# Edges and node tiles taken from the last to the first in a graph-attention and mixture-of-experts kernel

## The reference

```python
def reference(x, src, dst, ...):
    n = layernorm(x)
    h = (n @ W).reshape(N, 8, 256)                      # 8 heads
    a_src, a_dst = einsum(h, att_src), einsum(h, att_dst)
    e = leaky_relu(a_src[src] + a_dst[dst], 0.2)
    alpha = softmax of e over the edges of each dst      # max, exp, sum, divide
    x = x + segment_sum(h[src] * alpha, dst).mean(heads) + bias
    t = layernorm(x)
    probs = softmax(t @ router_w.T); the top 2 of 8 experts, weights normalised
    return x + t + sum over the two of weight * (gelu(t @ w1[e] + b1[e]) @ w2[e] + b2[e])
```

## Time and profile before

| | |
|---|---|
| median of three runs | 1113.08 us |
| the profiled execution | 1112.33 us, its span 1110.6 us |
| busy share PE, DVE, ACT, POOL | 64%, 62%, 32%, 60% |
| granted TensorE clock, mean | 0.81 |
| first gather, first block, last block, last projection | 75, 213, 725, 932 us |

### The profile page before, as it was taken

One profiled execution on the slowest core, in us unless ns is written; L12 is line 12 of the kernel. 1 busy time (PEld: TensorE's weight loads), 2 busy tenths in 40 slices (PEclk: granted clock), 3 DMA queues, 4 the chain that ended last, 5 costly groups with the idle time before them and its releaser, 6 DMA issues.

```text
span 1110.6 us, 16896 instructions
## 1 busy us (share of the span) xinstructions
PE 708.7 (64%) x3738; PEld 629.2 (57%) x3739; DVE 688.1 (62%) x1906; ACT 359.7 (32%) x833; POOL 664.9 (60%) x687
## 2 busy tenths in 40 slices
PE   1594002427565454756676666679999998669884
PEld 0593001317455444745566565568888888558774
DVE  6888008737574674667578676536768865735452
ACT  4800003000111122333464565543223222426553
POOL 1668778777777777777777700134063265556665
PEclk9855555578868787887886886789999998979998
DMA  9523143333444455665676748489876761455663
GB/s 347 170 52 86 50 101 98 104 109 105 138 126 139 144 153 165 190 197 173 213 249 202 237 172 326 160 298 354 332 291 220 274 241 64 107 110 94 103 106 47
DMA packets 97065, 190.12 MB, mean 171 GB/s; under 512 B 24745, under 2 KB 54772, under 8 KB 95848
## 3 DMA queue, kind: packets, MB, share of 16 engines
q0 software_dynamic: 31632, 70.45, 25.4%
q1 hardware_dynamic: 50236, 72.80, 19.2%
q10 hardware_dynamic: 15072, 45.36, 10.9%
HBM read 124.74 MB, written 64.74 MB: 171 GB/s over the span
## 4 chain that ended last, share of the span: by engine, by line
PE 27%; POOL 22%; issue 16%; DMA 11%; DVE 10%; ACTq 6%; ACT 6%; POOLq 2%; DVEq 0%; SPq 0%
POOL ring L670 19%; PE banks L879 11%; PE banks L1000 10%; DMA out<-ring 6%; ACTq L1150 5%; POOL starts_table L725 2%; PE banks L854 2%; ACT banks L1168 1%; ACT arena L1164 1%; ACT ring L1121 1%; DMA ring<-agg_table 1%; DMA agg_table<-arena 1%; DMA ring<-node_table,idx 1%; ACT banks L1170 1%; PE banks L1020 1%
## 5 line engine op out<-in xcount | busy, mean ns | idle before, releaser
L670 POOL DMA_INDIRECT ring<-node_table,idx x392 | 409.3, 1044 | 125.7 <-issue 114.8
L879 PE MATMUL banks<-arena,ring 128*128 128x160 f32 x1568 | 289.5, 350 | 125.2 <-issue 60.8
L879 PEld LDWEIGHTS banks<-arena,ring 128*128 128x128 f32 x1568 | 268.8, 228 | 147.0 <-issue 147.0
L1164 ACT COPY arena<-banks 128x400 f32<-128x400 f32 x200 | 88.3, 492 | 292.3 <-PE banks L879 148.1
L782 POOL DMA_INDIRECT out<-ring x56 | 88.5, 1581 | 61.0 <-DMA out<-ring 28.4
L1000 PE MATMUL banks<-ring 128*128 128x256 f32 x544 | 120.5, 381 | 0.0
L1000 PEld LDWEIGHTS banks<-ring 128*128 128x128 f32 x544 | 102.5, 190 | 13.4
L1609 DVE TENSOR_TENSOR arena<-hot,arena 128x640 f32<-128x640 f32 x98 | 75.1, 821 | 38.8 <-PE banks L879 38.4
L1168 ACT COPY banks<-zeros 128x400 f32<-128x400 f32 x100 | 49.5, 495 | 89.2 <-ACT arena L1164 52.2
L1059 PEld LDWEIGHTS banks<-ring 128*128 128x128 f32 x448 | 61.5, 203 | 14.6 <-DVE ring L1837 11.9
L1075 PE MATMUL banks<-arena,ring 128*128 x224 | 64.3, 413 | 7.6 <-issue 4.9
(11 more groups left out here) (374 smaller groups left out, 1106.3 us busy)
## 6 DMA issues: line engine op xcount, KB each, us to landing
agg_table<-arena ACTq DMA_DIRECT2D x100, 400.0 KB
ring<-agg_table SPq DMA_DIRECT2D x25, 1600.0 KB, 8.0
ring<-slot_table SPq DMA_DIRECT2D x56, 130.0 KB, 2.4
ring<-node_table,idx POOLq DMA_INDIRECT x392, 3.2
ring<-in_x SPq DMA_DIRECT2D x8, 640.0 KB, 14.7
arena<-in_L_ffn_w SPq DMA_DIRECT2D x16, 256.0 KB, 8.9
node_table<-ring SPq DMA_DIRECT2D x5, 640.0 KB, 5.1
out<-ring POOLq DMA_DIRECT2D x5, 512.0 KB, 4.3
```

The lines of the kernel that those rows point to most:

```text
L670: pool.indirect_dma_start(rows[:, b % ROOM, :], None, node_table, bass.IndirectOffsetOnAxis(idx[:, b:b + 1], 0)).then_inc(got[got_of(g)], 16)
L879: m = pe.matmul(columns[:, k, bass.ds(at * (UNIT * H), SPREAD * H)], lhs[:, k * P:(k + 1) * P], weights, start=False, stop=True, skip_grou ...
L1164: act.copy(stage[j][:, k * SLOTS * H:(k + 1) * SLOTS * H], views[k]).then_inc(drained, 1)
```

## The change

Every key is mirrored: an edge's destination becomes 3199 - dst (`MIRROR`), edges and tiles run from last to first. Homes 0 and 1 are then the empty ones, home 2 holds the padding and the last nodes, home 99 holds nodes 0 to 31. The edges are reversed within rows as they are read, and the table of destinations is written by an indirect store on POOL in place of a plain one on ACT. `aggt` is written with both inner dimensions reversed, so that tiles come out in the usual lane order. `rows_of(t)` = 24 - t gives the tile of nodes of step t. The step of 53 real nodes is now the first, so the first ten steps have 1205 real nodes in place of 1280, and `FIRST_JOBS` falls from 13 to 11; `job_lists`, `job_rows` and `job_experts` of round two each stand one result earlier.

```diff
-FIRST_JOBS = 13
+FIRST_JOBS = 11
-STORE = 4
+BASE_STORES = ((1, 5), (5, 9), (9, 13), (13, 17), (17, 20))
+    MIRROR = TILES * P - 1
+        def rows_of(t):
+            return TILES - 1 - t
 # SP
             load_nodes(0)
+            sp.wait_ge(node_pad, 1)
+            sp.dma_start(x_all[0:LAST_WHOLE, FULL, :], x[FULL * P:FULL * P + LAST_WHOLE, :]).then_inc(in_nodes[0], 16)
+            sp.dma_start(x_all[LAST_WHOLE:LAST, FULL, :], x[FULL * P + LAST_WHOLE:N, :]).then_inc(in_nodes[0], 16)
...
+            sp.wait_ge(base_ready, 1)
+            sp.dma_start(out[FULL * P:FULL * P + LAST_WHOLE, :], x_all[0:LAST_WHOLE, FULL, :]).then_inc(end_stored, 16)
+            sp.dma_start(out[FULL * P + LAST_WHOLE:N, :], x_all[LAST_WHOLE:LAST, FULL, :]).then_inc(end_stored, 16)
 # POOL
+            link(pool.tensor_scalar(node_keys[:, :], node_ids[:, :], -1.0, float(MIRROR), ALU.mult, ALU.add))
+            link(pool.iota(row_places[:, :], ...))
+            pool.wait_ge(keys_ready, 1)
+            pool.indirect_dma_start(dst_table.rearrange("(i n) -> i n", n=RUN), ..., dst_keys, None).then_inc(dst_stored, 16)
 # ACT
-            act.wait_ge(in_edges, 16 * 2 * (1 + TURN_ROWS - TURN_WHOLE))
-            act.dma_start(dst_table.rearrange("(i n) -> i n", n=RUN), edges_i[:, 1, :]).then_inc(dst_stored, 16)
-                         bank[h][:, 0:NB].rearrange("p (r i) -> p r i", r=TURN_BLOCKS)).then_inc(score_d_ready, 1)
+                         bank[h][:, 0:NB].rearrange("p (r i) -> p r i", r=TURN_BLOCKS)[:, :, ::-1]).then_inc(score_d_ready, 1)
-                to = aggt[t % AGG_RING].rearrange("p (k h) (v n) -> p k h v n", k=2, n=HOME)
+                to = aggt[t % AGG_RING].rearrange("p (k h) (v n) -> p k h v n", k=2, n=HOME)[:, :, :, ::-1, ::-1]
 # DVE
-            dve.tensor_copy(edges_f, edges_i).then_inc(edges_ready, 1)
+            link(dve.tensor_scalar(edges_f[:, 1, :], edges_i[:, 1, ::-1], -1.0, float(MIRROR), ALU.mult, ALU.add))
+            dve.tensor_copy(edges_f[:, 0, :], edges_i[:, 0, ::-1]).then_inc(edges_ready, 1)
+            dve.tensor_copy(dst_keys, edges_f[:, 1, :]).then_inc(keys_ready, 1)
...
+            link(dve.tensor_copy(starts_at[:, :], inside[:, 0, :]))
+            link(dve.tensor_single_scalar(starts_at[:, :], starts_at[:, :], 9, op=ALU.arith_shift_right))
+            link(dve.tensor_copy(block_of[:, :], starts_at[:, :]))
+            link(dve.scalar_tensor_tensor(inside[:, 0, :], block_of[:, :], -2.0 * RUN, inside[:, 0, :], ALU.mult, ALU.add))
+            link(dve.tensor_scalar(inside[:, 0, :], inside[:, 0, :], float((TURN_ROWS - 1) * RUN), None, ALU.add))
...
             results(5)
             count_jobs(1)
+            job_lists(1)
             results(6)
-            job_lists(1)
+            job_rows(1)
             results(7)
-            job_rows(1)
-            results(8)
             job_experts(1)
             dve.wait_ge(jobs_ready, 2)
-            for j in range(9, JOBS):
+            for j in range(8, JOBS):
                 results(j)
```

More of the change, by code:

```diff
@@ L110, in gat_moe_kernel @@
     ROUND_JOBS = (range(FIRST_JOBS), range(FIRST_JOBS, JOBS))
-    assert FIRST_JOBS <= -(-(2 * FIRST_TILES * P - NX * (P - 1)) // P) and FIRST_TILES % UNROLL == 0 and FIRST_TILES <= TN_RING
-    assert Y_RING * STORE == TILES - UNROLL
+    assert FIRST_JOBS <= -(-(2 * (FIRST_TILES * P - P + LAST) - NX * (P - 1)) // P) and FIRST_TILES % UNROLL == 0 and FIRST_TILES <= TN_RING
+    assert Y_RING == len(BASE_STORES) and BASE_STORES[-1][1] == TILES - UNROLL
     SLOT = D + 4
@@ L589, in _ @@
                 load_xs(j)
[L591 to L595, removed]
+            sp.wait_ge(base_ready, 2 * (TILES - UNROLL) + UNROLL)
+            sp.dma_start(out[0:UNROLL * P, :].rearrange("(t p) d -> p t d", p=P), x_all[:, 0:UNROLL, :]).then_inc(out_stored, 16)
             for j in range(XS_RING, FIRST_JOBS):
@@ L610, in _ @@
                 sp.wait_ge(y_sent[j % Y_RING], y_landed(j))
-            sp.wait_ge(out_stored, 16 * 3)
+            sp.wait_ge(out_stored, 16)
+            sp.wait_ge(end_stored, 32)
         @block.gpsimd
@@ L656, in _ @@
                                     pattern=[[1, P]], channel_multiplier=-1))
-            link(pool.affine_select(out=in_last[:, :], in_=ones_sq[:, 0:1], compare_op=ALU.is_gt, fill=0.0, base=LAST,
+            link(pool.affine_select(out=in_end[:, :], in_=ones_sq[:, 0:1], compare_op=ALU.is_gt, fill=0.0, base=LAST,
                                     pattern=[[0, 1]], channel_multiplier=-1))
@@ L789, in _ @@
                     base(t)
-                    if t % STORE == STORE - 1 and t // STORE < Y_RING:
-                        store_base(t // STORE)
+                    for i in range(Y_RING):
+                        if t + 1 == BASE_STORES[i][1]:
+                            store_base(i)
                 if q < TILES // UNROLL - 1:
@@ L1664, in add_node @@
                 dve.wait_ge(proj_done, t + 1)
-                dve.scalar_tensor_tensor(x_all[:, t, :], bank[proj_bank(t)][:, 0:D], 1.0 / H, x_all[:, t, :], ALU.mult, ALU.add)\
+                dve.scalar_tensor_tensor(x_all[:, rows_of(t), :], bank[proj_bank(t)][:, 0:D], 1.0 / H, x_all[:, rows_of(t), :], ALU.mult, ALU.add)\
                     .then_inc(y1_ready, 1)
                 dve.wait_ge(y1_ready, t + 1)
-                link(dve.bn_stats(stats[:, t, :], x_all[:, t, :]))
+                link(dve.bn_stats(stats[:, t, :], x_all[:, rows_of(t), :]))
             def normalise(t0, tiles):
@@ L1685, in normalise @@
                         dve.wait_ge(tT_ready, t - TN_RING + 1)
-                    dve.tensor_scalar(tn[t % TN_RING][:, 0:D], x_all[:, t, :], mean[:, t:t + 1], rstd[:, t:t + 1],
+                    dve.tensor_scalar(tn[t % TN_RING][:, 0:D], x_all[:, rows_of(t), :], mean[:, t:t + 1], rstd[:, t:t + 1],
                                       ALU.subtract, ALU.mult).then_inc(tn_ready, 1)
@@ L1724, in second_pick @@
                 link(dve.tensor_tensor(two, rev, bc(r[4], UNROLL), ALU.is_equal))
-                if tiles.stop == TILES:
-                    link(dve.tensor_scalar(one[:, UNROLL - 1, :], one[:, UNROLL - 1, :], in_last[:, 0:1], None, ALU.mult))
-                    link(dve.tensor_scalar(two[:, UNROLL - 1, :], two[:, UNROLL - 1, :], in_last[:, 0:1], None, ALU.mult))
+                if q == 0:
+                    link(dve.tensor_scalar(one[:, 0, :], one[:, 0, :], in_end[:, 0:1], None, ALU.mult))
+                    link(dve.tensor_scalar(two[:, 0, :], two[:, 0, :], in_end[:, 0:1], None, ALU.mult))
                 link(dve.tensor_tensor(A, one, two, ALU.add))
```

55 lines of the change are left out of this document (29 added, 26 removed).

## The result

The kernel after takes 1081.1 us (median of 4 runs, 1079.88 to 1083.42), the kernel before 1113.96 beside it (4 runs, 1111.56 to 1116.22). The ratio is 0.971, with an interval of 0.968 to 0.9735. The profiled execution took 1081.41 us with a span of 1079.7, 30.9 less than before's.

A forecast was written before the change was run, and what follows sets the result against it. Gathers bound until about 500 us, then the loop of DVE, PE and ACT, then PE. Terms 0.6, 0, -20.3, -8.1, 0 and +4.8 sum to -23.0 against 1112.33: 1089.3, so median 1090 us, range 1078 to 1108.

The forecast's parts named there:

- rival B: PE's quads reach 3.04 us, DVE's chain alone sets periods of groups 5 to 8: -12, 1078 us; chance 0.08.
- Start, and groups 0 to 5: Setup cast split into reversed operations: +0.6 us; early groups' drains stay covered by POOL's gathers: 0, +14 if cover fails.
- Groups 6 to 9: Late block stage: with few drains, alpha periods shorten by 3.9, 2.5, 3.6 and 8.0 us, within -20.3.
- Alpha of group 9 to the last block: Last group starts late after alpha for want of a bank; DVE's rescaling keeps it at 3.5 us: -2.3.
- From blocks to projection: After the last block only one home is left to drain: PE's pause -6.0, slow-clock start -2.1, together -8.1 us.
- Projection: Reversed writes in the projection windows cost nothing: 0; DVE has 48 us of room if they cost more.
- rival C: Reversed stores make DVE the bound of the projection, 1129 us at 2.3 times the store time; chance 0.06.
- Jobs: In the job rounds PE stands two jobs earlier and two more follow: +4.8 us, bounds +3.7 and +9.
- Against the occupancy: From 591 to 627 us ACT is least busy, 20.02 of 36 us; the busiest-engine rule says not to relieve it.

The follow-up runs named there:

- the slowed kernel: The kernel before with two idle ACT copies added to every drain: 1157.86 us, ratio 1.041.
- the jobs' part alone: The kernel before with 11 jobs in the first round in place of 13 and list operations one result earlier, nothing mirrored: 1117.28 us, ratio 1.0033.

## Why the prediction was right, and where its steps were not

*The number.* 1081.1 us lies in the stated range, but 9 us below the 1090 that was forecast and only 3 above rival B's 1078. B's mechanism gave little of that: it expected 12 us from shorter periods of groups 5 to 8, and the periods came out 3.7 us shorter than worked out. Another 4.3 us came from the jobs, and 0.9 and 0.8 from two stretches that were sized nearly right. Against these stand the 2.2 us of the one step that was wrong. These hid part of how far the rest was off, which is luck.

*Start, and groups 0 to 5: right.* Alpha of group 0 came 1.4 us late (0.6 predicted). Alpha of group 1 came 8.5 us late (7 predicted). The next wait for rows didn't make that good, as the prediction said: groups 2 and 3 were still 7.5 and 4.6 us late, and only by group 4 nothing of it was left. What the prediction didn't say is how near the edge that is: 72 drains in four groups are covered at 2.66 us each, and the kernel loses some 21 us when each takes 0.8 to 1 us more.

*Groups 6 to 9: right in mechanism, short in size.* The four periods came out 1.7, 0.6, 0.6 and 0.8 us shorter than worked out, which makes the 3.7 us of that term. The 3.55 us a quad, taken from rows in which some homes still end, is the likeliest of its parts: in the first period 12 quads in 46.6 - 5.7 = 40.9 us are 3.41 each. That four fifths of what is added to a drain of the late groups show up in the time of before is shown by the slowed kernel, and that from group 4 on in the kernel after little of it does (2.2 of 21 us) is shown too. No run made a drain cheaper by enough to show the same in the other direction. The split between quads and restart wasn't measured.

*Alpha of group 9 to the last block: wrong.* The step said that group 9 starts late "for want of a bank" and gave -2.3. The bank was free in the kernel after and the distance stayed: 5.5 us. What PE waits for is DVE's rescaling of the sums at the border (`rescaled`, L984 in the kernel before and L1002 after), which stands behind alpha and the spreads: it ends at 692.21 + 1.12 = 693.33 and the quad starts 2.63 us later. In ten other traces, of edits of both kernels, the quad follows the end of rescaling by 2.62 to 2.69 us, also where drains are slow. In the eight of them with the old order PE's idle time ahead of the quad is just as constant (5.5 to 5.6 us), so they don't single the rescaling out. The two with the rescaling first do: there the idle time falls to 4.1 us, and the 2.6 us stay. What fills these wasn't split. In the earlier trace rows the distance is 2.89 (rescaling ends at 715.37), and it is 2.91 in before with all drains slow, so the drain that the row names as releaser cost at most 0.3 us. Moving the rescaling ahead of alpha gains 0.4 us at most, since it must itself wait for PE to finish the group before (1.55 us, released by L1001). A wait for several semaphores had been read by the one that came last, and DVE's share taken as 3.5 without looking at what the first quad needs.

*From blocks to projection: right, -6.3 for -6.0.* The run without empty drains removes the pause alone. The slow start is gone too: project(2) takes 7.07 us for 32 records, where it took 9.24 (a difference of 2.2; 2.1 predicted). The granted clock in the first 14 us from its start was 0.85 before and is 1.00 after.

*Projection: right.* PE's 182.57 us are the same to the hundredth, DVE's 140.20 have 48 us of room, and rival C falls with the 981 and 1019 ns of the reversed stores.

*Jobs: the term of the sum that was mis-sized.* +4.8 was predicted and +0.5 came: round two is 3.3 us longer, and the stretch ahead of it 2.8 us shorter, which had been put at 0. In the jobs' part alone, with before's tokens, the two are +4.9 and -1.6. So the 4.8 for two jobs more hold there, and part of the 2.8 us goes with the earlier stand of PE alone; why round two grows by less in the kernel after stays open. There the 2.8 us are nearly all won early: from the first result to the fifth addition on POOL, behind which the last sends begin, 23.8 us passed before (935.58 to 959.34) and 21.3 after (904.20 to 925.46). With other tokens in the first jobs, two of these additions waited long for the transfer of the one ahead (3.84 and 3.12 us), and before three did (3.27, 2.66 and 3.12). In the jobs' part alone there were again three (3.11, 2.26 and 3.18), and 23.3 us passed. This is read from the traces of three kernels; no run changed the order of tokens by itself.

*Against the occupancy.* ACT was the least busy engine in 591 to 627 us, and over two thirds of its work went out of that window as the periods became shorter. The Trainium skill's rule (Perfetto Trace Analysis, Identifying the Most-Contended Engine) goes by occupancy and would have named POOL first. In the slowed kernel before, +44.5 us came from the engine with 20.02 of 36 us busy, while POOL's last gather stayed, so in this stretch a ranking by occupancy points to the wrong engine.

## What to carry to other kernels

Ask of each engine's work not how much there is, but where it stands: what was added to each drain came out to four fifths where the loop of three engines bounds, and hardly at all where the gathers do, until the drains came denser than the gathers. Work at a border between stages is judged by when its last transfer lands, so empty or trivial last steps belong ahead of it. Taking bytes out of a step proves nothing until the trace shows that the step itself became shorter.

## What was not expected of the hardware

A pair of clearings of 400 columns took 2 x 0.49 us, of 16 columns 2 x 0.17, and the cadence of drains went only from 2.66 to about 2.6 us. ACT's stand ahead of them, in which it loads three marks into registers, grew from 0.77 to 1.04 us (medians) and, with the 0.28 us that often follow the clearing, took most of the place; in the one drain without such loads there is no stand. A reversed fp32 store of 128x432 took 981 and 1019 ns in the two groups of operands, forward 1024 and 983: no cost. A single idle copy of 128x400 took 0.52 us (1.07 for the pair), but the pair lengthened a drain by 0.82 us only. Loading values into registers between two operations is thus part of a drain's cost here, though no row of the timeline shows it as work.
